# Selective-scan block: head pairs on the partition halves, x times step size in channel layout, dt bias by PE, a five-term softplus series, prefix sums in the x tap banks

## The reference, cut to what matters

```
z0, x0, z, xBC, dt = split(u @ in_proj_w.T)        # 64, 64, 64, 128, 4 columns
dt  = softplus(dt + dt_bias)
xBC = silu(causal 4-tap depthwise conv(xBC) + conv_b)
xs, Bm, Cm = split(xBC)                            # 64, 32, 32; 4 heads of 16
h_t = h_{t-1} * exp(-exp(A_log) * dt_t) + dt_t * x_t * B_t ;  y_t = h_t @ C_t
y   = rmsnorm((y + D * x) * silu(z)) * norm_w
out = concat(silu(z0) * x0, y) @ out_proj_w.T
```

## Time and profile before

| | |
|---|---|
| median of 3 runs | 72.57 us |
| the profiled execution | 72.53 us, of it 70.7 us span |
| PE busy | 59.8 us (85%), 1014 matmul instructions |
| DVE / ACT / POOL busy | 51.7 / 30.4 / 27.8 us |
| mean granted TensorE clock | 0.952 of full |
| mixer proper | from 12 to 50 us of the span |

### The profile page before, as it was taken

One profiled execution on the slowest core, in us unless ns is written; L12 is line 12 of the kernel. 1 busy time (PEld: TensorE's weight loads), 2 busy tenths in 40 slices (PEclk: granted clock), 3 DMA queues, 4 the chain that ended last, 5 costly groups with the idle time before them and its releaser, 6 DMA issues.

```text
span 70.7 us, 2413 instructions
## 1 busy us (share of the span) xinstructions
PE 59.8 (85%) x1014; PEld 39.3 (56%) x1016; DVE 51.7 (73%) x143; ACT 30.4 (43%) x71; POOL 27.8 (39%) x63
## 2 busy tenths in 40 slices
PE   2999989999969999969089999999989789695910
PEld 1335449664963337951079993994866734293700
DVE  1073286885839998999999939997438589999740
ACT  0260785824289157360628001216593700687100
POOL 5997489305774005107999881000006005000000
PEclk9999999999999999999996555999999999999999
DMA  0999700000000000000000000000000000000034
...
DMA packets 1869, 2.74 MB, mean 39 GB/s; under 512 B 193, under 2 KB 1217, under 8 KB 1858
## 3 DMA queue, kind: packets, MB, share of 16 engines
...
q10 hardware_dynamic: 578, 1.02, 4.1%
...
## 4 chain that ended last, share of the span: by engine, by line
PE 27%; DVE 20%; issue 4%; POOLq 2%; ACT 1%; DVEq 1%; ACTq 0%
PE ps L487 6%; PE ps L511 4%; PE ps L502 4%; PE ps L521 3%; DVE x2b L917 2%; PE ps L538 2%; PE ps L606 2%; DVE ell L883 2%; POOLq L84 2%; PE ps L529 1%; DVE qc L1071 1%; DVE xdz L907 1%; DVE qb L1073 1%; DVE h L1074 1%; DVE h L1055 1%
## 5 line engine op out<-in xcount | busy, mean ns | idle before, releaser
L290 PE MATMUL ps<-zbf 128*128 128x512 bf16 x39 | 12.0, 463 | 1.6 <-DVE zbf L805 1.3
L883 DVE TENSOR_TENSOR_SCAN ell<-ps,delta 128x512 f32<-128x512 f32 x8 | 9.2, 1206 | 0.9 <-PE ps L385 0.9
L290 PEld LDWEIGHTS ps<-zbf 128*128 128x128 bf16 x41 | 4.3, 115 | 7.8 <-issue 4.2
L606 PE MATMUL ps<-h,wk 64*64 64x256 bf16 x144 | 4.7, 274 | 1.6 <-DVE h L1074 0.9
L606 PEld LDWEIGHTS ps<-h,wk 64*64 64x64 bf16 x144 | 3.9, 106 | 2.6 <-issue 2.3
L930 DVE TENSOR_TENSOR mm<-ell,gsb 128x1024 f32<-128x1024 f32 x4 | 4.7, 1210 | 0.0
L487 PEld LDWEIGHTS ps<-mm,xdz 64*32 64x32 f32 x256 | 4.2, 133 | 0.9 <-issue 0.8
L487 PE MATMUL ps<-mm,xdz 64*32 64x64 f32 x256 | 4.6, 268 | 0.0
L337 PE MATMUL ps<-u,wtap 64*64 64x512 f32 x32 | 4.4, 614 | 0.0
L385 PEld LDWEIGHTS ps<-rows,sel 96*128 96x128 bf16 x32 | 2.0, 97 | 4.2 <-DVE ell L883 2.6
L1194 POOL TENSOR_TENSOR sc<-sc 128x1 f32<-128x1 f32 x1 | 0.2, 190 | 10.3 <-ACT sc L743 10.3
...
...
## 6 DMA issues: line engine op xcount, KB each, us to landing
...
```

Source lines behind the costliest of these rows:

```text
L290: mul(ps[:, bank, :], zbf[:, 0:P], zbf[:, :], start=True, stop=True)
L606: last = mul(ps[col:col + CH, CONV[turn] + far, 0:TOK], wk[row:row + CH, tap, :], src[row:row + CH, b, dy:dy + SIDE, dx:dx + SIDE], start= ...
L883: vec_.tensor_tensor_scan(dst, ps[:, SPREAD[g % 2], :], delta[:, :], 0.0, ALU.mult, ALU.add).then_inc(scanned, 1)
```

## The change

- **Layout.** Where a 128-partition tile held two 64-token chunks, its two partition halves now hold the two heads of a pair for one chunk. `inner_products` gets a stationary operand of 32 rows by 128 columns (B twice, from `bc2`, made on POOL) and runs as (j, p); j = 0 goes to banks 2 and 3, j = 1 to banks 4 and 7. `mm` is multiplied straight out of PSUM, so ACT's copy `gsb` is gone. `inside` contracts over 128 rows and needs half as many matmuls, each alone in its columns (no accumulation).
- **x times dt** is made in channel layout: POOL copies dt wide (`dtv`), PE moves it to channels (`channel_steps`, 4 f32 matmuls twice), ACT copies it out (`dtc`), POOL multiplies (`xd`), and the transposes take `xd` in place of `xc`. DVE loses L893, L895 and the four L907; ACT fills `xdz` with eight copies instead, each four once DVE has finished with the bank of that j (`x2_ready` 3 and 6).
- **dt bias** is added by a K = 1 matmul into the bank of `dt_proj`; |v| is taken on ACT. ACT's `spread_of(0)` moves behind it, `spread_of(1)` behind `lxb`.
- **Series** with five coefficients, was seven: two DVE instructions fewer.
- **Prefix sums** go to banks 0 and 1, the last two behind the rows matmuls; `x_projection(0)`, which stood ahead of the sums, comes after spread 1, and taps 1 to 3 one spread later.
- **PE order.** The z gate now comes ahead of the products and in banks 2 and 3; the x0 gate comes after the state. `gated_share(0)` comes after all of `inside`, behind four `keep_warm`.

The diff, cut to its core:

```diff
...
-SERIES = [float(c) for c in np.polyfit(_z, np.arctanh(_s) / _s, 6)]
+SERIES = [float(c) for c in np.polyfit(_z, np.arctanh(_s) / _s, 4)]
...
-        LXB, SPREAD, GB, ZB, XTB, BTB = (5, 6), (5, 6), (2, 3), (2, 3), (0, 1), 4
-        HB, YI, YA, SSQ, RB, PO = 4, (5, 6), ((0, 1), (2, 3)), (0, 2), ((1, 3), (0, 2)), (4, 7, 5, 6)
-        SE, OSUM, CONV = (0, 1), (1, 3), (2, 5)
+        LXB, SPREAD, ZB, XTB, BTB, DTC = (0, 1), (5, 6), (2, 3), (0, 1), 4, 7
+        GB, X0B, NORM, HB, YI, YA = ((2, 3), (4, 7)), (5, 6), 3, 0, (1, 2), (3, 4)
+        SSQ, RB, PO = (1, 2), ((3, 1), (4, 2)), (7, 0, 5, 6)
+        SE, OSUM, CONV = (4, 1), (2, 3), (2, 5)
...
+            mul(ps[:, DTB, 0:IH].rearrange("p (i h) -> p i h", h=HEADS), onesq[0:1, :],
+                vc[0:1, V_DTB:V_DTB + HEADS].unsqueeze(1).broadcast_to([1, TILES, HEADS]), start=True, stop=False)
...
-            x_projection(0)
...
+            def prefix(j, *ts):
+                for t in ts:
                     at = HEADS * (8 * j + 2 * t)
                     last = mul(ps[:, LXB[j], P * t:P * t + P], dtw[:, at:at + 8, :].rearrange("p i d -> p (i d)"), upto[:, :],
                                start=True, stop=True)
-                last.then_inc(prefix_sums, 1)
+                return last
+            pe.wait_ge(dt_wide, 1)
+            prefix(0, 0, 1, 2, 3).then_inc(prefix_sums, 1)
+            prefix(1, 0, 1)
...
+            prefix(1, 2, 3).then_inc(prefix_sums, 1)
+            def channel_steps(j):
+                for t in range(4):
+                    at = HEADS * (8 * j + 2 * t)
+                    last = mul(ps[:, DTC, P * t:P * t + P], dtv[:, at:at + 8, :].rearrange("p i d -> p (i d)"), ident, start=True, stop=True)
+                last.then_inc(dtc_ready, 1)
+            pe.wait_ge(w_copy, 1)
+            pe.wait_ge(dtv_ready, 1)
+            channel_steps(0)
...
+            def inner_products(j, p):
+                for k in range(2):
+                    for c2 in range(2):
+                        for b in range(2):
+                            s = slice(64 * p + 32 * b, 64 * p + 32 * b + 32)
+                            c = 2 * k + c2
+                            col = CHUNK * (4 * k + 2 * p + c2)
+                            last = mul(ps[:, GB[j][b], col:col + CHUNK], bc2[s, j, c, :, :].rearrange("n e t -> n (e t)"),
+                                       csilu[s, j, CHUNK * c:CHUNK * c + CHUNK], start=True, stop=True, tile_position=(s.start, 0))
...
-            pe.wait_ge(lxb_ready, 2)
             pe.wait_ge(rows_sb, 1)
             spread_rows(0)
             spread_rows(1)
+            pe.wait_ge(lxb_ready, 2)
+            x_projection(0)
+            spread_rows(2)
             x_projection(1)
-            spread_rows(2)
+            spread_rows(3)
             x_projection(2)
-            spread_rows(3)
+            spread_rows(4)
             x_projection(3).then_inc(xs_proj, 1)
-            spread_rows(4)
             pe.wait_ge(mxr_ready, 1)
-            mul(ps[0:CH, STAT, 80:81], one_row, mxr[:, :], start=True, stop=True)
-            mul(ps[CH:P, STAT, 80:81], one_row, mxr[:, :], start=True, stop=True).then_inc(w_mm, 1)
+            mul(ps[0:CH, DTB, 80:81], one_row, mxr[:, :], start=True, stop=True)
+            mul(ps[CH:P, DTB, 80:81], one_row, mxr[:, :], start=True, stop=True).then_inc(w_mm, 1)
+            pe.wait_ge(dtc_sb, 1)
+            channel_steps(1)
...
             x_to_tokens(0)
-            x_to_tokens(1)
             spread_rows(6)
+            pe.wait_ge(w_copy, 2)
             for j in range(2):
                 for k in range(2):
                     last = nc.tensor.transpose(ps[:, BTB, P * (2 * j + k):P * (2 * j + k) + P], bc[:, j, P * k:P * k + P], ident)
             last.then_inc(bt_ready, 1)
+            x_to_tokens(1)
             spread_rows(7)
             pe.wait_ge(z0_silu, 2)
-            for b in range(2):
-                inner_products(0, b)
-            for b in range(2):
-                pe.wait_ge(g_half, b + 1)
-                inner_products(1, b)
+            gate(ZB, wa_sb[:, A_Z:A_Z + CH], z_proj)
+            pe.wait_ge(bt_sb, 1)
+            pe.wait_ge(dtc_sb, 2)
+            pe.wait_ge(bc2_ready, 1)
+            inner_products(1, 0)
+            pe.wait_ge(g_half, 1)
+            inner_products(1, 1)
+            pe.wait_ge(silu_z, 2)
             pe.wait_ge(w_pool, 1)
             pe.wait_ge(w_stats, 2)
-            mul(ps[:, STAT, 96:99], half_ones, sc[:, 8:11], start=True, stop=True).then_inc(w_mm, 1)
-            pe.wait_ge(g_sb, 2)
-            gate(ZB, wb_sb[:, B_X0:B_X0 + CH], x0_proj)
-            pe.wait_ge(scanned, 8)
-            gate(SPREAD, wa_sb[:, A_Z:A_Z + CH], z_proj)
-            pe.wait_ge(bt_sb, 1)
+            mul(ps[:, NORM, 96:99], half_ones, sc[:, 8:11], start=True, stop=True).then_inc(w_mm, 1)
+            pe.wait_ge(w_copy, 3)
+            inner_products(0, 0)
+            pe.wait_ge(g_half, 2)
+            inner_products(0, 1)
             pe.wait_ge(x2_ready, 6)
+            pe.wait_ge(xd_ready, 4)
...
+            pe.wait_ge(scanned, 8)
+            gate(X0B, wb_sb[:, B_X0:B_X0 + CH], x0_proj)
...
+                for k in range(2):
+                    for c2 in range(2):
+                        for p in range(2):
+                            for r in range(2):
+                                q0 = 64 * p + 32 * r
+                                col = TOK * b + P * k + CHUNK * c2
+                                last = mul(ps[q0:q0 + 32, YA[j], col:col + CHUNK], xdz[:, tile(j, b, k, p), c2, r, :, :],
+                                           mm[:, 2 * j + b, 4 * k + 2 * p + c2, r, :], start=True, stop=True, tile_position=(0, q0))
...
-            pe.wait_ge(xd_ready, 4)
-            pe.wait_ge(m_ready, 1)
+            pe.wait_ge(m_ready, 2)
             inside(0, 0)
-            pe.wait_ge(m_ready, 2)
             inside(0, 1).then_inc(ya_ready, 1)
+            pe.wait_ge(w_pool, 2)
+            mul(ps[:, HB, 448:450], half_ones, sc[:, 16:18], start=True, stop=True).then_inc(w_mm, 1)
+            pe.wait_ge(m_ready, 4)
+            inside(1, 0)
+            inside(1, 1).then_inc(ya_ready, 1)
             pe.wait_ge(gated0, 4)
             pe.wait_ge(w_copy, 4)
+            keep_warm(4, PO[0])
             gated_share(0)
-            pe.wait_ge(m_ready, 3)
-            inside(1, 0)
-            pe.wait_ge(m_ready, 4)
-            inside(1, 1).then_inc(ya_ready, 1)
             pe.wait_ge(zero_eps, 1)
+            pe.wait_ge(yd_ready, 2)
             squares(0)
-            pe.wait_ge(ydx_ready, 2)
             gated_share(1)
-            keep_warm(2, YA[0][1])
...
+            act.wait_ge(dt_proj, 1)
+            go(dta[:, :], ps[:, DTB, 0:IH], ACT.Abs).then_inc(dt_neg, 1)
+            act.wait_ge(dt_neg, 1)
+            go(dtb[:, :], dta[:, :], ACT.Exp, scale=-1.0).then_inc(dt_exp, 1)
...
+            def channel_steps(j):
+                act.wait_ge(dtc_ready, j + 1)
+                go(dtc[:, 2 * j:2 * j + 2, :], ps[:, DTC, :].rearrange("p (b t) -> p b t", b=2), ACT.Copy).then_inc(dtc_sb, 1)
+            channel_steps(0)
...
-            g_by_b = gsb[:, :, :].rearrange("p (j b i) t -> p b j (i t)", j=2, b=2)
-            for b in range(2):
-                act.wait_ge(g_ready, b + 1)
-                go(g_by_b[:, b], ps[:, GB[b], :].rearrange("p (j c) -> p j c", j=2), ACT.Copy).then_inc(g_sb, 1)
-            act.wait_ge(w_mm, 3)
-            go(sc[:, 12:15], ps[:, STAT, 96:99], ACT.Copy).then_inc(w_copy, 1)
             act.wait_ge(z_proj, 1)
             for j in range(2):
-                go(sz[:, BANK * j:BANK * j + BANK], ps[:, SPREAD[j], :], ACT.Silu).then_inc(silu_z, 1)
+                go(sz[:, BANK * j:BANK * j + BANK], ps[:, ZB[j], :], ACT.Silu).then_inc(silu_z, 1)
+            act.wait_ge(zero_xdz, 1)
+            for j in range(2):
+                act.wait_ge(x2_ready, 3 * j + 3)
+                for c2 in range(2):
+                    for e in range(2):
+                        heads = ps[half(c2), XTB[j], :].rearrange("s (i r e d) -> s i r e d", r=2, e=2, d=HDIM)
+                        go(xdz[half(e), 8 * j:8 * j + 8, c2, :, e, :], heads[:, :, :, e, :], ACT.Copy).then_inc(xd_ready, 1)
+            act.wait_ge(w_mm, 3)
+            go(sc[:, 12:15], ps[:, NORM, 96:99], ACT.Copy).then_inc(w_copy, 1)
...
-            for c in SERIES[1:4]:
-                seal(stt(dtp[:, :], dtp[:, :], c, dtz[:, :], ALU.add, ALU.mult))
-            for c in SERIES[4:-1]:
+            for c in SERIES[1:-1]:
...
-            dve.wait_ge(g_sb, 2)
             blocks(0, 0)
             blocks(0, 1)
             blocks(1, 0)
+            blocks(1, 1)
...
+            gp.tensor_scalar(dtv[:, :, :], wide(dt[:, :], HDIM), 1.0, 0.0, ALU.mult, ALU.add).then_inc(dtv_ready, 1)
...
+            pool.wait_ge(b_silu, 1)
+            gp.tensor_scalar(bc2[:, :, :, :, :].rearrange("n j c e t -> n (j c) e t"),
```

(19 more changed lines are left out.)

127 lines of the change are left out of this document (40 added, 87 removed).

## The result

The changed kernel takes 81.53 us, median of four executions (80.26 to 84.26), against 72.96 for the kernel before on the same chip: a ratio of 1.1155, 95% interval 1.108 to 1.123. That is slower, as forecast, but far beyond the 74.8 and beyond the upper end of the range, 76.8. Some executions of every kernel here carry low clock beyond that of the kernel's quickest ones: medians include them, ratios leave them out, and the profiled launches of the changed kernel (84.26, its longest) and of e4, e5, e6, e7, f1 and a1 are among those left out.

What follows compares the result with a forecast made beforehand. The prediction took PE's chain, part of it at low clock, as the mixer's bound and DVE as second. Head gain, later scans, the wait for products and low-clock PE work put the squares at 52.5 against 50.24: 72.5 + 2.3 = 74.8 us, range 72.7 to 76.8.

Steps and rivals of the forecast that it cites:

- So I expect the low clock again until about 44.3: PE's granted clock falls to 0.50 after an idle of some 2.4 us (about 34 to 36.5) and recovers about 44.3.
- Head, "gains 0.45": dt ready at 15.8 instead of 16.53, spreads starting at 20.4 to 20.5 instead of 20.85: a gain of 0.45 us.
- Scans, idle of 2.25 before the sixth: DVE idles 2.25 us before the sixth scan, released by PE; last scan ends at 32.35 against 30.84, +1.5.
- POOL's product, "from above I take 1.04": POOL's `xd` takes between half of 1.04 and 1.04 us; both done by 29.5, ahead of the transposes: costs nothing.
- x side: DVE's x side behind the scans takes 2.5 us and ends at 34.95, as before (35.02).
- Copies: Four ACT `xdz` copies behind `x2_ready` 6 take 1.2 to 1.3 us, so `w_copy` 3 comes at 36.5.
- Products, 1.7 for 32 passes: PE's products of j = 0 take 0.053 a pass, ready at 38.2; DVE idles 3.25 us waiting for them.
- rival 2: 128-column product loads run one by one: products end at 40.55, squares at 54.0, +3.8, total 76.3 us; chance 0.2.
- `blocks` out of PSUM at 1.14: DVE's four `blocks` take 1.14 us each, 4.55 in all; reading one operand from PSUM costs nothing.
- Rival 1: Products cheap or clock holds: at full clock 73.1 us with products at 0.8, 74.0 with 1.7; chance 0.25.
- product passes of 0.03 or 0.12: Sign that the forecast is wrong: PE's product passes at these times, where it took 0.053 a pass.
- Rival 3: DVE never waits for the products and goes on at 34.95: squares end at 48.4, -1.8, total 70.7 us; chance 0.1.

Runs made afterwards that it cites:

- e4: Changed kernel with the statistics matmul behind all products in bank 5, no product waiting for `w_copy` 3, DVE taking j = 1 first: 77.16 us, ratio 1.0572.
- e5: e4 with six `keep_warm` matmuls between the tiny matmul and the state: 74.44 us; the one execution a ratio would count took 72.59.
- e6: e4 with the tail order of the kernel before, `gated_share(0)` inside `inside(1)`, no `keep_warm(4)`, ACT's second square earlier: 74.39 us; one countable execution 72.28.
- e7: e4 with POOL's wide copy `dtv` held back until DVE has finished its split into parts: 76.08 us, ratio 1.048.
- f1: e6 with four `keep_warm` between the products of j = 1 and j = 0 and three behind them: median 74.31 us, ratio 1.0023.
- a1: b1 plus the change's head alone (dt bias by PE, Abs on ACT, five coefficients), prefix sums not moved: median 75.87 us, ratio 0.998.
- Experiment 8: Two runs: b1, the kernel before with fillers in PE's idle stretch, ratio 0.982; and a1, b1 plus the change's head alone, ratio 0.998.
- experiment 2: Run e2: changed kernel with 13 matmuls of zeros in PE's idle stretch ahead of the wait for `w_copy` 3: 78.8 us, ratio 1.0835.
- experiment 4: Run e5: e4 with six `keep_warm` between the tiny matmul and the state: 74.44 us.
- e1: Changed kernel with ACT's copy that raises `w_copy` to 3 moved ahead of the eight `xdz` copies: 77.97 us, ratio 1.0595.
- e2: Changed kernel with 13 matmuls of zeros in PE's idle stretch ahead of the wait for `w_copy` 3, the wait kept: 78.8 us, ratio 1.0835.
- experiment 3: Run e4: changed kernel with no product waiting for `w_copy` 3 and DVE taking j = 1 first: 77.16 us, ratio 1.0572.
- experiments 1, 2 and 3: The runs e1, e2 and e4, in that order, each an edit of the changed kernel: ratios 1.0595, 1.0835 and 1.0572.
- b1: Kernel before the change with 7 matmuls of zeros in PE's idle stretch at 33.5 to 35.2: 71.26 us, ratio 0.982.

## Why the prediction went wrong

The direction and the place were right, the size was not: 81.5 for 74.8. The step that failed most is "So I expect the low clock again until about 44.3": the clock stayed at 0.50 until 54.5, so nearly all of PE's work behind the idle time ran at half rate. Next to it, the products were priced as if at full clock, and the split as if POOL did nothing beside it. Step by step, in the profiled execution:

- **Head, "gains 0.45": wrong.** dt came 0.54 sooner counted from `rstd`, for the 0.7 worked out. Then the split, taken at its old length, met POOL's new wide copy: 0.72 lost on one line. So the first scan came at 21.68, for 20.9 worked out and 21.34 before. Experiment 8 shows that the softplus part of the head, without the moved prefix sums, gives next to nothing. What failed is the sentence on the split "2.86 behind dt", which had no look at what POOL does beside it.
- **Scans, idle of 2.25 before the sixth: right.** 2.40, released by the sixth spread; last scan's end 33.29 for 32.35, 0.8 of it from the head.
- **POOL's product, "from above I take 1.04": wrong bound.** 1.27 each. It cost nothing on the path, as said.
- **x side: right** in length (2.5), 0.8 late.
- **Copies: mis-sized.** 0.40 each, within the bounds of 0.25 to 0.5, but the first four were not done when `x2_ready` 6 came: they start at 34.61, so all eight run in one row, and `w_copy` 3 comes 2.2 behind the x side and not 1.55: +0.7.
- **Products, 1.7 for 32 passes: mis-sized by 2.3.** At full clock a pass takes 0.071 (2.28, experiment 2), +0.6. The estimate of 3.4 that was worked out from the Trainium skill, "TensorE: Matmul & The Clock Gate", section "LDWEIGHTS (loading the stationary operand)", with loads one behind the other, was too high: the trace has 2.28 for these alternating row groups. (It would also stand 0.65 under rival 2's 4.06, and not within 0.5 of it.) How long one of these loads takes by itself no run here shows. The other 1.7 is the clock, which the prediction had low from here on and yet priced the products at full rate. That is an error within its own working: an expected 0.50 was applied to the state and not to the products ahead of it.
- **`blocks` out of PSUM at 1.14: right** (4.61 for four).
- **"The low clock again until about 44.3": wrong, and the largest term.** The clock was low from 37.5 to 54.5. From the end of the products to the end of the squares PE needed 17.6 for the 14.3 worked out. At full clock the estimate of 1.2 for `inside` would have been good (1.10 and 1.20, experiment 4); it took 1.94, twice. Low y from the state 2.81 for 2.5, tiny matmul 0.5 for 0.25, `keep_warm` with its idle 1.7 for 0.9. I took the time of the recovery from the kernel before, where a gated share stood between the two `inside`. Here that share had been moved behind both, and nothing between the idle time and 53 raised the clock, the x0 gate neither; e6, with the share back, had it up at 47.8. That the share did it is argued from where the clock rose: e4, without it, was back at 49.2.
- **The sum.** 0.8 (x side) + 0.7 (copies) + 2.3 (products) + 3.3 (PE behind them) is 7.1: 59.7 for 52.5. That nothing changes behind the squares was right: from their end to the end of the span it takes 20.5 before and 20.5 in e1, e2, e6 and e7, whose clock was full there. In the profiled launch of the changed kernel another 2.4 arose there; two more low stretches lie in its second half in the same row of the page, and the 16 `keep_warm` ahead of the first conv stretched to set its start:

```profile
61.65 1.98 PE L551 MATMUL ps<-cs,rr 128*64 128x128 f32 x16
...
68.59 5.09 PE L295 MATMUL ps<-zbf 128*128 128x512 bf16 x16
73.60 2.25 PE L627 MATMUL ps<-h,wk 64*64 64x256 bf16 x72
```

- **The rivals.** Rival 1 fell. Rival 2 had the time of the products (4.0) by the wrong cause, and its sign came with it ("product passes of 0.03 or 0.12"; they took 0.125): a sign read as a time, without the clock beside it, would have confirmed it. Rival 3's mechanism, DVE without a gap, was made in experiment 3, and did not end at 70.7 but at 77.2: it had DVE's time nearly right (second gated y 13.2 behind the x side, for the 11.5 worked out) and PE's wrong. No rival and no bound of the range held "low clock for the whole of the mixer's tail".

What stays open: what in a stretch of small matmuls brings the clock down while PE is shown busy, as in experiments 1, 2 and 3. It does not do so each time: the execution of e5 that took 72.59 had a mean granted clock of 1.00 with the same 64 product passes. In the profiled f1 and b1, with fillers among the small matmuls, it stayed at 1.00 up to the second squares; a1, with the fillers of b1, still had two low stretches, at other places. And how much the clock and the order are worth apart is open, since e5 and e6 have one execution each that counts.
